# A transformer block's attention scores: two-part fp32r operands on four row tiles of 32 in place of three-part bf16 on two of 64, raw products five beats ahead instead of seven, and a reordered prologue

## The reference

```python
def _tc_rmsnorm(x, t, gw, gb, bw, bb):
    g, b = (t @ gw.T + gb)[:, None, :], (t @ bw.T + bb)[:, None, :]
    return g * x * lax.rsqrt(mean(x * x, -1, keepdims=True) + EPS) + b
q, k, v = ((x @ W.T).reshape(B, L, 16, 8) for W in (Wq, Wk, Wv))
p = softmax(einsum('blhd,bmhd->bhlm', q, k) / sqrt(8), axis=-1)
attention = einsum('bhlm,bmhd->blhd', p, v).reshape(B, L, D) @ Wo.T
swiglu = (silu(x @ gate_w.T) * (x @ hid_w.T)) @ out_w.T      # hidden size 512
x1 = x + attention(norm(x)); y = x1 + swiglu(norm(x1)); result = x + y
```

## Time and profile before

| | us |
|---|---|
| median of 3 runs | 257.99 (257.29 to 258.37) |
| profiled execution, its own time | 255.85 |
| its span | 254.0 |
| PE busy | 223.3 (88%) |
| DVE busy | 203.0 (80%) |
| ACT busy | 163.4 (64%) |
| POOL busy | 112.0 (44%) |
| mean granted TensorE clock | 0.993 |

### The profile page before, as it was taken

One profiled execution on the slowest core, in us unless ns is written; L12 is line 12 of the kernel. 1 busy time (PEld: TensorE's weight loads), 2 busy tenths in 40 slices (PEclk: granted clock), 3 DMA queues, 4 the chain that ended last, 5 costly groups with the idle time before them and its releaser, 6 DMA issues.

```text
span 254.0 us, 8307 instructions
## 1 busy us (share of the span) xinstructions
PE 223.3 (88%) x3084; PEld 180.8 (71%) x3084; DVE 203.0 (80%) x490; ACT 163.4 (64%) x352; POOL 112.0 (44%) x183
## 2 busy tenths in 40 slices
PE   3496677779989999999989999999999999899894
PEld 2384454457668868786878877877787878687893
DVE  4648866888898989889888998899888997564673
ACT  5355748867865786569756776667757655666430
POOL 8324852695283345526282526152623232324310
PEclk9999979999999999999999999999999999999999
DMA  5867602510360026001530054004500000000001
GB/s 166 343 169 169 169 4 65 156 45 5 85 170 1 27 66 186 26 24 40 156 85 18 11 151 122 4 26 128 147 3 26 1 26 3 23 3 25 22 23 41
DMA packets 18819, 18.79 MB, mean 74 GB/s; under 512 B 3644, under 2 KB 17980, under 8 KB 18652
## 3 DMA queue, kind: packets, MB, share of 16 engines
q1 hardware_dynamic: 18252, 17.80, 24.9%
q10 hardware_dynamic: 528, 0.46, 0.8%
HBM read 3.22 MB, written 2.10 MB: 21 GB/s over the span
## 4 chain that ended last, share of the span: by engine, by line
PE 43%; issue 24%; POOL 16%; DVE 6%; ACT 4%; SPq 3%; ACTq 1%; DMA 1%; POOLq 0%; DVEq 0%
PE proj L489 7%; PE pv L427 6%; PE ffn L320 5%; PE score L410 4%; PE ffn L322 3%; PE ffn L321 3%; SPq L254 3%; POOL inv L933 3%; PE raw L383 2%; POOL qp L925 2%; PE tok L442 2%; POOL xn_lo L946 2%; POOL kp L925 2%; POOL xs L939 2%; POOL xn_lo L918 2%
## 5 line engine op out<-in xcount | busy, mean ns | idle before, releaser
L766 DVE TENSOR_REDUCE nmax<-raw 128x8 f32<-128x1024 f32 x61 | 74.2, 1217 | 2.8 <-PE raw L383 2.6
L607 ACT ACTIVATE p_s<-score 128x1024 f32<-128x1024 f32 x64 | 65.4, 1022 | 17.1 <-PE score L410 15.9
L427 PE MATMUL pv<-p_s,va 128*32 128x128 f32 x1024 | 41.7, 280 | 1.9 <-ACT xn L625 1.2
L320 PE MATMUL ffn<-xn_hi,ffn_hi 128*128 128x256 f32 x106 | 34.8, 328 | 1.2 <-POOL xn_lo L946 1.2
L636 ACT ACTIVATE th<-ffn 128x256 f32<-128x256 f32 x53 | 20.4, 384 | 19.6 <-PE ffn L322 19.6
L489 PE MATMUL proj<-ffn_out_s,hT 128*128 128x128 f32 x240 | 31.6, 275 | 0.0
L823 DVE SCALAR_TENSOR_TENSOR gated<-th,ffn 128x256 f32<-128x256 f32 x53 | 22.0, 415 | 12.0 <-ACT th L636 11.7
L427 PEld LDWEIGHTS pv<-p_s,va 128*32 128x32 f32 x1024 | 24.7, 109 | 9.3 <-issue 4.1
L946 POOL TENSOR_TENSOR xn_lo<-xn,xn_hi 128x128 fp32r<-128x128 f32 x32 | 14.7, 460 | 34.6 <-DVE xn_hi L814 34.6
L322 PE MATMUL ffn<-xn_hi,ffn_lo 128*128 128x256 f32 x106 | 29.7, 280 | 0.0
L321 PE MATMUL ffn<-xn_lo,ffn_hi 128*128 128x256 f32 x106 | 29.6, 279 | 0.0
(11 more groups left out here) (132 smaller groups left out, 469.2 us busy)
## 6 DMA issues: line engine op xcount, KB each, us to landing
ks<-kp SPq DMA_DIRECT2D x48, 128.0 KB, 2.4
qs<-qp SPq DMA_DIRECT2D x45, 128.0 KB, 2.5
out_y<-x_s SPq DMA_DIRECT2D x16, 128.0 KB, 1.8
x_s<-in_x SPq DMA_DIRECT2D x1, 1536.0 KB, 10.0
qs<-shift SPq DMA_DIRECT2D x64, 4.0 KB
x_s<-in_x SPq DMA_DIRECT2D x2, 256.0 KB, 3.5
ffn_in_s<-in_ffn_in_w SPq DMA_DIRECT2D x1, 512.0 KB, 6.7
qs<-qp ACTq DMA_DIRECT2D x3, 128.0 KB, 3.7
```

What stands on the lines that cost most here:

```text
L320: pe.matmul(dst, w_hi, v_hi, start=True, stop=False)
L427: mm = pe.matmul(pv[VW * j:VW * j + VW, (t % 2) * L:(t % 2 + 1) * L], va[vbuf(g)][:, t // 2, at:at + VW], p_s[:, (BEATS * g + t) % PBUF, p ...
L607: act.activation(p_s[:, n % PBUF, :], score[:], ACT.Exp, scale=SCALE).then_inc(s_exp, 1)
L766: dve.tensor_reduce(heads[:, :, t % 2, :], raw_dst(g, t)[:].rearrange("l (e j m) -> l e j m", e=HALVES, j=HQ), AX.X, ALU.max, negate=True) ...
```

## The change

- Two fp32r parts instead of three bf16 parts (`PARTS` 2, three part pairs). A head's rows are 8 x 3 = 24 (laid out with a stride of 4), the shift is one fp32 row (31), and a row tile has 32 rows. The four row tiles are 2 (t % 2) + e: even beats use tiles 0 and 1, odd beats 2 and 3. `qs` and `ks` hold 4 heads in fp32 instead of 8 in bf16, the same bytes.
- `a_middle`, `a_lowest`, the second shift instruction and `lowest_first` are gone; `a_rest` becomes `a_low` and writes the second part.
- RAW -7 becomes -5, MAXT -3 becomes -2. From beat 3 on, score of beat T and raw of beat T + 5 are issued alternately (`c_score_and_raw`), after both their waits. Beats 0 to 2 keep them apart, raw behind PV; the first raw products are made in alternating pairs (`b_raw_two`).
- The maxima's transpose goes into `raw` instead of `pv`, after xt2 instead of before the first norm's transpose; the next raw product waits for the shift's copy.
- Group 0's first half is shifted batch by batch (`b_first_maxT`, `b_first_shift`, `first_shift_rows`), the transfers placed between the stack transfers of group 1. The first key is made in two halves.
- V of group 0 moves forward in the prologue, V of group 1 from beat 1 to beat 5. Group 2's first norm and its split move into the prologue. `tok` and `ffn` become halves of `aux`, which also takes three early raw products. Eight unread products follow in beat 2 and four in beat 3, behind a wait for the seventh maximum.
- Some work moves between engines: V's zero fill from DVE to POOL, from ACT's prologue into beat 1; the FFN weights' split into the prologue; the query stack's first transfers from three on ACT to one each for K and Q there.

The diff, cut to its core:

```diff
-    PARTS = 3
-
-    Q_PART = [0, 0, 0, 1, 1, 2]
-    K_PART = [0, 1, 2, 0, 1, 0]
+    PARTS = 2
+    TROWS = 32
+    STRIDE = 4
+
+    Q_PART = [0, 0, 1]
+    K_PART = [0, 1, 0]
...
-    RAW, MAXT = -7, -3
+    RAW, MAXT = -5, -2
+    FIRST_VALUE = 5
+    APART = 3
...
-    SPREAD = BEATS * G + RAW + 1 - FFN
+    SPREAD = BEATS * G + MAXT + 1 - FFN
...
+        shift = sb("shift", [MROWS, 2, L], F32R)
+        shift_first = sb("shift_first", [H, MB, L], F32R)
...
+        aux = bank("aux", 1024)
+        ffn, tok = aux[:, 0:512], aux[:, 512:1024]
...
-        def tile_rows(e, n):
-            return slice(HALF_ROWS * e, HALF_ROWS * e + n)
+        def tile_rows(e, t, n):
+            at = TROWS * (2 * (t % 2) + e)
+            return slice(at, at + n)
...
-            return score if g == 0 and t % 2 and t < BEATS - 1 else raw
+            return (raw, score, aux, raw, aux, raw, aux, raw)[t] if g == 0 else raw
+
+        def raw_free(g, t):
+
+            return BEATS * g + t if g > 0 else (0, 0, 0, 1, 3, 4, 5, 6)[t]
+
+        def first_maxT(b):
+            return proj[0:H, 0:L] if b == 0 else pv[0:H, 3 * L:4 * L]
...
             def shift_rows(g, half):
 
+                sp.wait_ge(s_shift, 2 * g + half if g > 0 else half)
                 for b in range(MB):
-                    for i, ready in enumerate((s_shi, s_slo)):
-                        sp.wait_ge(ready, 2 * g + half + 1)
-                        sp.dma_start(qs[buf(g)][SHIFT + i::HALF_ROWS, :, (MB * half + b) * L:(MB * half + b + 1) * L],
-                                     shift[H * b:H * (b + 1), half, i, :]).then_inc(
-                                         s_shiftrow[buf(g)][MB * half + b], 16)
+                    sp.dma_start(qs[buf(g)][SHIFT::TROWS, :, (MB * half + b) * L:(MB * half + b + 1) * L].bitcast(F32),
+                                 shift[H * b:H * (b + 1), half, :].bitcast(F32)).then_inc(
+                                     s_shiftrow[buf(g)][MB * half + b], 16)
+
+            def first_shift_rows(b):
+                sp.wait_ge(s_shift0, b + 1)
+                sp.dma_start(qs[0][SHIFT::TROWS, :, b * L:(b + 1) * L].bitcast(F32),
+                             shift_first[:, b, :].bitcast(F32)).then_inc(s_shiftrow[0][b], 16)
...
                 stack_rows(g, ks, kp, K_PART, 0, s_khi)
...
+                stack_rows(g, ks, kp, K_PART, 1, s_klo)
+                stack_rows(g, qs, qp, Q_PART, 0, s_qhi)
+                stack_rows(g, qs, qp, Q_PART, 1, s_qlo)
...
-            stack(0)
-            stack(1)
-            shift_rows(0, 0)
+            one_rows(0)
+            one_rows(1)
+            sp.wait_ge(s_khi, 1)
+            sp.dma_start(ks[0][0::STRIDE, :, :].rearrange("p j w -> p (j w)").bitcast(F32),
+                         kp[:, 0, 0, :].bitcast(F32)).then_inc(s_stack[0], 16)
+            stack_rows(0, ks, kp, K_PART, 1, s_klo)
+            sp.wait_ge(s_qhi, 1)
+            sp.dma_start(qs[0][1::STRIDE, :, :].rearrange("p j w -> p (j w)").bitcast(F32),
+                         qp[:, 0, 0, :].bitcast(F32)).then_inc(s_stack[0], 16)
+            stack_rows(0, qs, qp, Q_PART, 1, s_qlo)
+            stack_rows(1, ks, kp, K_PART, 0, s_khi)
+            first_shift_rows(0)
+            stack_rows(1, ks, kp, K_PART, 1, s_klo)
+            stack_rows(1, qs, qp, Q_PART, 0, s_qhi)
+            stack_rows(1, qs, qp, Q_PART, 1, s_qlo)
+            first_shift_rows(1)
...
+            def first_key():
+
+                pe.wait_ge(s_wlo, 1)
+                for n in range(2):
+                    half = slice(2 * n * L, 2 * (n + 1) * L)
+                    pe.wait_ge(s_lo1, n + 1)
+                    mm = split_product(key_dst(0)[:, half], qk_hi[:, 1, :], qk_lo[:, 1, :], xn1_hi[:, half],
+                                       xn1_lo[:, half])
+                mm.then_inc(s_k, 1)
...
+            def raw_ready(g, t):
                 if t == 0:
                     pe.wait_ge(s_stack[buf(g)], stacked(g))
-                if g == 0:
+                    if g < NBUF:
+                        pe.wait_ge(s_onerows[g], 16)
+                if g == 0 and t == 0:
+                    pe.wait_ge(s_xn1, 2 * NB)
+                if g == 0 and t == 2:
+                    pe.wait_ge(s_qlo, 1)
+                if raw_free(g, t) > 0:
+                    pe.wait_ge(s_max, raw_free(g, t))
+                if g > 0 and t % HQ == 0:
+                    pe.wait_ge(s_shift, 2 * g - 1 + t // HQ)
+
+            def raw_pair(g, t, e, j):
+                return pe.matmul(raw_dst(g, t)[:, pair_cols(e, j)],
+                                 qs[buf(g)][tile_rows(e, t, RAW_ROWS), j, batch_cols(t)],
+                                 ks[buf(g)][tile_rows(e, t, RAW_ROWS), j, batch_cols(t)], start=True, stop=True)
...
+            def score_ready(g, t):
+                if g == 0 and t < HQ:
+                    if t % 2 == 0:
+                        pe.wait_ge(s_shiftrow[0][t // 2], 16)
                     if t == 0:
-                        pe.wait_ge(s_xn1, 2 * NB)
-                    if t == BEATS - 1:
-                        pe.wait_ge(s_max, t)
...
+            def b_raw_two(g, t):
+
+                raw_ready(g, t)
+                raw_ready(g, t + 1)
+                for j in range(HQ):
+                    for e in range(HALVES):
+                        first = raw_pair(g, t, e, j)
+                        if j == HQ - 1 and e == HALVES - 1:
+                            first.then_inc(s_raw, 1)
+                        second = raw_pair(g, t + 1, e, j)
+                second.then_inc(s_raw, 1)
...
+            def c_score_and_raw(g, t, f, r):
+
+                score_ready(g, t)
+                raw_ready(f, r)
+                for j in range(HQ):
+                    for e in range(HALVES):
+                        mm = score_pair(g, t, e, j)
+                        if j == HQ - 1 and e == HALVES - 1:
+                            mm.then_inc(s_score, 1)
+                        nn = raw_pair(f, r, e, j)
+                nn.then_inc(s_raw, 1)
...
+            def b_maxT(g, half):
+                pe.wait_ge(s_max, BEATS * g + HQ * (half + 1))
+                pe.transpose(raw[:, 0:L], nmax[g % 2][:, half * 128:half * 128 + 128],
+                             ident[:]).then_inc(s_maxT, 1)
+
+            def b_first_maxT(b):
+                pe.wait_ge(s_max, 2 * (b + 1))
+                if b == 0:
+                    pe.wait_ge(s_va, 1)
+                else:
+                    pe.wait_ge(s_klo, 2)
+                pe.transpose(first_maxT(b), nmax[0][:, H * b:H * (b + 1)], ident[:]).then_inc(s_maxT0, 1)
...
+            a_values(0)
+            unread_products(pv, 14)
+            b_raw_two(0, 0)
             a_key(1)
+            pe.wait_ge(s_va, 1)
+            unread_products(proj, 6)
+            b_raw_two(0, 2)
+            unread_products(proj, 4)
+            b_first_maxT(0)
+            for b in range(NB):
+                a_transpose(2, b)
             a_query(1)
-            b_raw(0, 0)
-            b_raw(0, 1)
-            unread_products(4)
-            b_raw(0, 2)
-            unread_products(4)
-            b_raw(0, 3)
-            unread_products(4)
-            b_raw(0, 4)
-            b_maxT(0, 0)
-            b_raw(0, 5)
-            a_transpose(2, 0)
-            a_transpose(2, 1)
-            a_values(0)
-            a_transpose(2, 2)
-            b_raw(0, 6)
-            a_transpose(2, 3)
+            pe.wait_ge(s_klo, 2)
+            unread_products(pv, 8)
...
                 for g, t in due(T, 0, BEATS):
-                    c_score(g, t)
-                for g, t in due(T, RAW, BEATS):
-                    b_raw(g, t)
+                    if T >= APART and due(T, RAW, BEATS):
+                        c_score_and_raw(g, t, *due(T, RAW, BEATS)[0])
+                    else:
+                        c_score(g, t)
+                if T == 0:
+                    b_first_maxT(1)
+                    b_raw_two(0, HQ)
                 for g, t in due(T, PV, BEATS):
                     c_pv(g, t, T)
+                if 0 < T < APART:
+                    for g, t in due(T, RAW, BEATS):
+                        b_raw(g, t)
...
+                if T == 2 or T == 3:
+                    pe.wait_ge(s_max, BEATS - 1)
+                    unread_products(ffn, 8 if T == 2 else 4)
...
-                dve.tensor_copy(shift[:, half, 0, :], pv[0:MROWS, 3 * L:4 * L]).then_inc(s_shi, 1)
-                dve.wait_ge(s_shi, 2 * g + half + 1)
-                dve.tensor_tensor(shift[:, half, 1, :], pv[0:MROWS, 3 * L:4 * L], shift[:, half, 0, :],
-                                  ALU.subtract).then_inc(s_slo, 1)
+                dve.tensor_copy(shift[:, half, :], raw[0:MROWS, 0:L]).then_inc(s_shift, 1)
+
+            def b_first_shift(b):
+
+                dve.wait_ge(s_maxT0, b + 1)
+                dve.tensor_copy(shift_first[:, b, :], first_maxT(b)).then_inc(s_shift0, 1)
...
```

(31 more changed lines are left out.)

283 lines of the change are left out of this document (111 added, 172 removed).

## The result

The change makes the kernel a little slower: median 259.88 us (257.86 to 265.54, 20 runs) against 257.26 (256.08 to 258.57, 20 runs) for the kernel before, ratio 1.0085 with 95% interval [1.006, 1.0111]. The forecast was 250.0, clearly faster. The profiled execution took 260.13, its span is 258.3 against 254.0.

A forecast was written before the change was run, and what follows sets the result against it. PE was taken to bound the steady beats. From the profiled 255.85 us, -10.0 - 0.6 + 1.2 + 1.6 = -7.8 gave 248.0; the runs' median standing 2.1 higher made it 250 us, range 241 to 272.

The forecast's parts named there:

- signs of being right: Beat 4's score near 34 us, score-raw pair 0.5 to 0.65, beats 3.1 to 3.3, tail 24, loads repeating under 35 ns.
- The prologue up to beat 4: Before beat 4: earlier stack transfers and shift rows bring beat 4 at 34.2 instead of 44.25 us, -10.0 us.
- From there to beat 4 DVE sets the pace: Prologue after first raw: DVE's eight maxima and other work take 11.6 us, from 19.4 to 31.0.
- the move of V: V of group 1 goes from the second to the sixth beat: 0.9 us of PE at most.
- Score and raw: PE, each beat: sixteen fp32r products on four tiles cost 0.54 us against 0.55 now, -0.6 us in the sum.
- The transpose in its own beat: Every fourth beat, next score waits for the maxima's transpose and copy: 0.1 us each, bounds 0 and 0.5, +1.6 us.
- The look-ahead: Late beats: raw five beats ahead instead of seven, FFN's further banks five beats later: +1.2 us, between 0.6 and 3.
- B: Rival, score and raw: short fp32r product costs each tile twice fp32's, pair 0.99 us, 273 us; chance 0.18.
- C: Rival, score and raw: loads of different tiles queue, pair 1.88 us, 330 us; chance 0.07.
- D: Rival, score and raw: four tiles pay, pair 0.33 us, 241 us; chance 0.12.
- E: Rival: early start given back through transpose waits of 0.5 us at 16 halves, or DVE's maxima; 258 us; chance 0.08.

The follow-up runs named there:

- e1: Kernel after, with the 1.95 us zero fill of V's second buffer moved from ACT in beat 1 to POOL: 259.45 us, ratio to before 1.0111.
- e3: Kernel after, with each beat's eight score products ahead of its eight raw products instead of alternating: 259.3 us, ratio to before 1.009.
- e4: Kernel after, with 56 more unread products on PE in beats 1, 2 and 4 to 9: 255.24 us, ratio to before 0.9933.
- f2: e4 with V's zero fill on POOL and raw product 7 joined to score 2: 257.76 us over four runs, 253.71 to 260.83.
- f4: Kernel before, with only V of the second group moved from beat 1 to beat 5: 259.0 us, ratio to before 1.0084.
- g1: Kernel before, with 62 unread products behind PV in beats 0 to 9: 258.45 us, ratio to before 1.0057.
- f1: e4 with DVE's row maximum ahead of its other work in beats whose maxima are transposed: 253.76 us, ratio to before 0.9892.
- e2: Kernel after, without the twelve unread products of beats 2 and 3: 258.44 us, ratio to before 1.0022.
- g2: e4 with f1's and f2's edits and the FFN's two further banks from beat 59: 253.18 us, ratio to before 0.9873.

## Why the prediction was wrong, point by point

The profiled execution took 260.13 us where the sum gives 248.0. Of these 12.1 us 8.7 lie ahead of beat 4 and 4.0 in beats 4 to 63, which I had at +2.2 in all and which take 6.2 more; the tail gives 0.7 back. Of the signs of being right only the first failed: the pair is 0.59, a beat 3.25 on average, the products repeat after 27.5 ns, but beat 4 is not near 34.

**The prologue up to beat 4** was given -10.0 us and brought -1.4. The step that failed is "From there to beat 4 DVE sets the pace". Its start came out right: first raw 19.12 (said 19.0), beat 0 at 25.00 (near 25). The 19.0 is partly luck: the stack went at 346 GB/s in place of 241, from 13.5 to 18 us instead of from 12.7 on, and the product began 1.1 us after that; in e1, e3 and e4 it began at 18.3. But the eight maxima don't follow each other. The eighth stands behind raw 7, that behind PV of beat 2, and that behind a score which waits for a norm behind a 1.95 us zero fill on ACT; it ended at 35.25 where my sum had all of DVE's work done at 31.0. Score of beat 4 came at 42.88 rather than 34.2. Of these 8.7 us, about 3.1 go with the clock: e4's beat 4 is 3.9 earlier, 0.8 of it from before beat 0. The others are handovers and unread products in their way; e1 puts 1.0 us on the fill and f2 1.0 on the join.

**The clock** stands in none of my terms, and this is what made the sign wrong. I costed the move of V at 0.9 us of PE work and not at the cover that it took from beat 1; f4 shows 0.84% for it, about 2.2 us, with the low stretch three times as long; about half of that stands in beats 0 to 4, where the low stretch is. The earlier trace rows and the mean clock of 0.993 in the profile of before were read as "full", while the thin beats just after the prologue were already down for 3.4 us. Without the two low stretches, and with 56 products more, the kernel after gains 1.5 points of ratio (1.0085 to 0.9933), about 4 us. That is what is left after paying for the products. The line through its executions puts it at 252.3 to 253.7 us without low stretches and without added products, 3.6 to 5 us under the kernel before as it ran and 2 to 4 above the forecast; this is an estimate, no run shows it. Nor does a run show the two designs at full clock alike in all else: e4's 254.6 and the 254.7 and 254.8 of the kernel before (two executions, mean clock 1.000) agree, but e4 has 56 products more in it, and the kernel before with 62 more (g1) takes 257.6 to 258.0.

**Beats 4 to 10** I took as ordinary. They take 15.5 us before, 20.5 after and 19.0 in e4. In them are V of group 1 (0.9 us in f4), the transposes' waits and the second low stretch; in e4 also 36 unread products. The early start is given back there, and how much each of the others takes is not separated.

**Score and raw** cost 0.59 with the switch against 0.54 forecast and 0.55 before; the mechanism (each tile repeats after 0.11 us, others beside it) is what the trace shows. The mis-sized part is 0.05 us a pair, or 3 us over the 60 beats. What I left out is the lone score when no raw is left to pair: 0.59 (225.69 to 226.28) against 0.33, in the last five beats some 1.3 us. Against this stand savings in the steady beats: 16 to 48 take 106.3 us against 106.7. That the lighter DVE pays for the dearer pair there is argued, not tested.

**The transpose in its own beat** I gave 0.1 us each. In the short beats it is more: from beat 50 to 51 3.02 against 2.35, 54 to 55 3.13 against 2.36, 58 to 59 3.30 against 2.44, so 0.7 to 0.9 in each of these, above my bound of 0.5. Neighbouring beats return part of it; over 48 to 56 the loss is 0.6. In the long beats nearly nothing is lost: over the whole kernel PE waits for the shift copy ahead of a score eight times, 0.24 us each (185.68 above is one), 2.0 us together. f1, which shortens just this chain, gains 1.0 us of span.

**The look-ahead** was priced at +1.2 for beats 57 and 58. Beats 56 to 59 take 9.02 against 8.05, with one of the transposes above in them; no run separates the two.

**The rivals.** B (a slow short product) and C (loads in a queue) would need pairs of 0.99 and 1.88 us; the pair is 0.59. That also decides against the Trainium skill's figures (TensorE: Matmul & The Clock Gate, "LDWEIGHTS (loading the stationary operand)") applied as a queue: four products with their loads start within 0.11 us. D (0.33) falls too. E, the early start given back, is what happened (258 said for it, 259.9 measured), though by another mechanism than its words: neither DVE nor the transposes in the main, but a chain of handovers at half clock. Its sign, a wait for the shift copy of more than 0.2 us at every fourth beat, came at eight of the sixteen. I gave it 0.08, so its number was met by luck.

**Two readings of the kernel before** were off, and nothing in the sum rests on them: beat 0 needs four maxima, so seven raw products were three more and not four, and 21 of the 24 stack transfers stood in SP's queue ahead of the shift rows, since three were issued by ACT.

**Open.** What makes the clock fall isn't worked out here. A thin stretch alone doesn't: in the earlier trace rows PE is busy 0.47 of 2 us and the clock is at 1.00. Why it falls a second time at 53.2 us, behind a stretch half idle (the kernel before keeps its clock there with PE busy 1.32 of 2 us from 50 to 52 and 1.36 from 54 to 56), is read from one profile only and isn't tested beyond e4. Open too are why the mean clock of one kernel differs between its executions (0.921 to 0.971 in e2, 0.967 to 1.000 in f2), the V move undone in the kernel after, and what each piece of g2 adds.

## What to carry to other kernels

Work taken out of PE, or moved between its beats, is priced by the clock in the stretch that it leaves, and not by its own duration: look in fine stretches at the clock of the thinnest beats before moving anything out of them. A chain across engines that was hidden by look-ahead (maximum, transpose, copy, score) needs its slack checked in the shortest beat, not in the mean one. When products are added or taken out, compare executions at the same mean clock: the cost of the products and the gain in clock can hide each other in a median, as in e2. Where an early start is forecast, follow each later beat's releaser in the program's order; "engine X sets the pace" holds only if its inputs stand ahead of what waits.

## What the runs showed of the hardware that I had not expected

- fp32r products of 128 columns on 32-row tiles run side by side: four start every 0.11 us, 27.5 ns each, while each tile repeats after 0.11. It happens without alternating the tiles in the program: in e3 a later product on a free tile started 0.03 us after the first.
- The clock stays down long after PE is busy again: 0.50 for 10.2 us, though from 36 to 38 us PE was busy 2.00 of 2 us, and 1.83, 1.41, 2.00 and 1.87 in the four stretches from 54 to 62. Unread products in the gaps removed this in the kernel after (-1.5 points) and cost 0.6% in the kernel before, where it was only 3.4 us long.
- A clock row of 1.00 doesn't yet mean full pace at the start. In the kernel after, fp32r products of 512 columns follow each other after 0.43 us at 11.5 to 12.4 us and after 0.24 us at 20.1 us, with the row at 1.00 in both places.
- Stack transfers of twice the size went faster. The first fill of the kernel after against the earlier trace rows (241 GB/s, DMA share 1.09):

```profile
14.00:16.00 2.00, 2.00 (x12) 2.00 (x11) 0.85 (x3) 1.70 (x5) 0.49 (x1) 1.00 1.02 367
16.00:18.00 2.00, 1.35 (x12) 1.15 (x10) 1.00 (x2) 1.45 (x9) 1.60 (x4) 1.00 0.93 343
```

  367 and 343 GB/s with the DMA engines as busy; over the kernel 11203 packets instead of 18819 move the same 18.79 MB. By the profile's page a stack transfer of 256 KB lands 2.5 to 2.8 us after its issue, one of 128 KB in the kernel before 2.4 to 2.5. The packets' size and the number of transfers changed together, so which of them it is isn't shown.
